# The first feed-forward block in pieces between the half images of the window attention

## What is computed

```python
h = _layernorm(x, ln1_w, ln1_b)                       # windows of 8 x 8
qkv = hw @ qkv_w + qkv_b                              # 12 heads of 8
attn = softmax(q @ k.T * scale + bias)                # per head and window
x = shortcut + (attn @ v) @ proj_w + proj_b
m = _layernorm(x, ln2_w, ln2_b)
m = gelu(m @ mlp_w1 + mlp_b1) @ mlp_w2 + mlp_b2       # 96 -> 384 -> 96
return x + m
```

## Time and profile before

| | us |
|---|---|
| median of three runs | 1312.41 |
| lowest and highest | 1305.92, 1313.32 |
| the profiled execution, its time | 1309.46 |
| its span | 1307.7 |
| window attention, from the start to 188.96 | 188.96 |
| first feed-forward program, 188.96 to 247.25 | 58.29 |
| conv mixer, 247.25 to 411.15 | 163.90 |

### The profile page before, as it was taken

How to read it: one execution, slowest core, us unless ns; L and a number is a source line. 1 busy time by engine, 2 the same in 40 slices (tenths; PEclk the granted TensorE clock), 3 DMA queues, 4 the chain that set the end, 5 groups by cost and what they waited for, 6 DMA issues and landing times. The chain is left out here.

```text
span 1307.7 us, 23695 instructions
## 1 busy us (share of the span) xinstructions
PE 1154.8 (88%) x8859; PEld 790.6 (60%) x8859; DVE 740.0 (57%) x2112; ACT 515.9 (39%) x839; POOL 387.1 (30%) x584
## 2 busy tenths in 40 slices
PE   4888879789887979999999997788888978999998
PEld 2565656566665656766666674466455544577776
DVE  3788844477772436666666666276455565333322
ACT  1555533343431333333343332345343422455543
POOL 3645445443425421010101210424100000353522
PEclk8999969899997989999999998699799999999999
DMA  4500000000000000000000000000000000000000
GB/s 88 100 11 2 2 2 0 1 1 1 2 1 1 0 1 1 1 1 1 1 1 1 1 2 1 1 1 1 1 2 1 2 2 1 2 13 7 9 11 13
DMA packets 28924, 9.39 MB, mean 7 GB/s; under 512 B 26961, under 2 KB 28816, under 8 KB 28816
## 3 DMA queue, kind: packets, MB, share of 16 engines
q1 hardware_dynamic: 25760, 7.02, 2.6%
q10 hardware_dynamic: 3056, 0.92, 0.3%
HBM read 6.36 MB, written 1.57 MB: 6 GB/s over the span
## 5 line engine op out<-in xcount | busy, mean ns | idle before, releaser
L156 POOL TENSOR_TENSOR ln_v<-MV,eps 128x2 f32<-128x2 f32 (+3 forms) x81 | 16.2, 201 | 427.2 <-PE bank L1132 247.3
L1194 ACT ACTIVATE fa_e<-bank 128x1024 f32<-128x1024 f32 x64 | 65.5, 1024 | 161.1 <-PE bank L1102 161.1
L1997 PEld LDWEIGHTS bank<-e_w,ex_G 128*128 128x128 f32 x768 | 90.6, 192 | 14.4 <-issue 14.1
L2112 DVE SCALAR_TENSOR_TENSOR X<-bank,ex_L,X 128x96 f32<-128x96 f32 x128 | 31.8, 311 | 114.0 <-PE bank L1997 108.1
L1246 DVE TENSOR_REDUCE fa_z<-bank 128x4 f32<-128x1024 f32 x64 | 78.3, 1223 | 26.3 <-PE bank L1084 24.7
L1989 PE MATMUL bank<-hT,e_w 96*128 96x512 f32 x192 | 90.6, 609 | 0.0
L1997 PE MATMUL bank<-e_w,ex_G 128*128 128x96 f32 x768 | 90.0, 274 | 0.0
L2040 ACT ACTIVATE ex_G<-bank,e_b 128x512 f32<-128x512 f32 x96 | 64.3, 686 | 61.7 <-PE bank L1989 58.9
L1844 DVE TENSOR_REDUCE ca_z<-bank 128x2 f32<-128x256 f32 x96 | 48.9, 552 | 49.3 <-PE bank L1571 49.2
L1102 PE MATMUL bank<-fa_a,fa_b 64*128 64x256 f32 x512 | 74.1, 409 | 1.1 <-DVE fa_a L1253 1.1
L1115 PE MATMUL bank<-fa_e,fa_v 128*64 128x256 f32 x512 | 72.0, 404 | 1.1 <-ACT fa_e L1194 1.1
(11 more groups left out here) (252 smaller groups left out, 2641.7 us busy)
## 6 DMA issues: line engine op xcount, KB each, us to landing
out_tokens<-X SPq DMA_DIRECT2D x8, 192.0 KB, 2.1
X<-in_x SPq DMA_DIRECT2D x56, 24.0 KB
e_w<-in_L_ffn_w SPq DMA_DIRECT2D x2, 576.0 KB
bias0r<-in_L_conv_rpb_table ACTq DMA_DIRECT2D x16, 24.0 KB
m0w<-in_L_conv_mlp_w SPq DMA_DIRECT2D x2, 144.0 KB
m1w<-in_L_conv_w SPq DMA_DIRECT2D x2, 144.0 KB
f_w<-in_L_ffn_W SPq DMA_DIRECT2D x2, 142.5 KB
mixer<-in_mixer SPq DMA_DIRECT2D x1, 256.0 KB
```

The source lines that it names most:

```text
L1194: act.activation(E[v % 2][:], k.banks[:, b:b + 2, :].rearrange("p i (c q) -> p i c q", c=2), ACT.Exp).then_inc(s["exp"], 1)
L1997: last = pe.matmul(bank[4 + e % 2][:, t * C:(t + 1) * C], G[e % 2][:, j, t * P:(t + 1) * P], k.ew2[:, e, j, :], start=(j == 0), stop=(j == ...
```

## The change

The feed-forward block's program disappears. Its work is written as four generators (`mlp_in_pieces`), whose next piece each engine's stream of the window attention calls at fixed places. From step 10 on, four steps of the attention (r = 0 to 3) hold one step m of the feed-forward block; the loop now runs to step 41. The pieces share one PSUM bank (6) and one G buffer; `probs_t` puts both of its groups into bank 2 instead. All engines wait for the late weights before step 10, GpSimd already after step 6. All statistics but those of the remaining `mlp` program are written by `bn_aggr` straight into MV, without the copy.

```diff
-def statistics(dve, k, s, n, count):
+def statistics(dve, k, s, n, count, first=0, unrolled=True):
...
+    if unrolled:
+        for t in range(count):
+            last = dve.bn_aggr(k.MV[:, n * count + t, :], k.stats[:, first + t, :])
+        last.then_inc(s["mv"], 1)
+        return
...
+def mlp_in_pieces(k, bank, ctx, prefix, w, prev):
...
+    def gpsimd(pool):
+        for i in range(IMAGES):
+            pool.wait_ge(prev["mv"], i + 1)
+            t = 4 + 2 * (i % 2)
+            normalise(pool, k, s, i, 2, k.Y[i // 2 % 2][:, t:t + 2, :], w["b2"], i // 2 - 1, 2 * i)
+            yield
...
+    def tensor(pe):
+        for m in range(steps):
+            pe.wait_ge(s["y"], 2 * m + 2)
+            after(pe, s["x"], m)
+            for t in range(4):
+                last = pe.transpose(bank[0:C, t * P:(t + 1) * P], k.Y[m % 2][:, 4 + t, :], k.ident[:])
+            last.then_inc(s["T"], 1)
+            yield
+            pe.wait_ge(s["hT"], m + 1)
+            for j in range(KH):
+                if j:
+                    pe.wait_ge(s["gelu"], KH * m + j)
+                pe.matmul(bank[:], w["w1"][:, j * P:(j + 1) * P], k.hT[m % 2][:], start=True, stop=True).then_inc(s["up"], 1)
+                yield
+            pe.wait_ge(s["gelu"], KH * (m + 1))
+            for t in range(4):
+                for j in range(KH):
+                    last = pe.matmul(bank[:, t * C:(t + 1) * C], G[:, j, t * P:(t + 1) * P], w["w2"][:, j, :], start=(j == 0), stop=(j == KH - 1))
+                if t == 1:
+                    yield
+            last.then_inc(s["down"], 1)
+            yield
+
+    def scalar(act):
+        for m in range(steps):
+            after(act, s["down"], m)
+            for j in range(KH):
+                act.wait_ge(s["up"], KH * m + j + 1)
+                act.activation(G[:, j, :], bank[:], ACT.Gelu, bias=w["b1"][:, j:j + 1]).then_inc(s["gelu"], 1)
+                yield
+
+    def vector(dve):
+        for m in range(steps):
+            dve.wait_ge(s["T"], m + 1)
+            after(dve, s["up"], KH * (m - 1))
+            dve.tensor_scalar(k.hT[m % 2][:], bank[0:C, :], w["g"][:], w["b"][:], ALU.mult, ALU.add).then_inc(s["hT"], 1)
+            yield
+            dve.wait_ge(s["down"], m + 1)
+            dve.wait_ge(s["xb"], 2 * m + 2)
+            add_new(dve, k, s, m, 4, bank[:, 0:4 * C].rearrange("p (t c) -> p t c", t=4))
+            yield
+            statistics(dve, k, s, m, 4, 2)
+            yield
...
@@ GpSimd
+                for u in range(HALVES + 6):
+                    if u < HALVES:
+                        pool.wait_ge(s["mx"], u + 1)
...
                     if u % 2 == 0 and u // 2 + 3 < IMAGES:
                         norm(u // 2 + 3)
-                pool.wait_ge(s["late"], 16 * len(k.late))
-                next_first_step(pool, k, s, IMAGES)
+                    if u == 6:
+                        pool.wait_ge(s["late"], 16 * len(k.late))
+                    if u % 2 == 1 and u >= 7:
+                        next(behind)
...
@@ TensorE, probs_t
-                    after(pe, s["pte"], 2 * u - 1 + b)
+                    after(pe, s["pte"], 2 * u + b)
...
@@ TensorE, the loop
                     if 0 <= u - 2 < HALVES:
                         probs_t(u - 2, 0)
                     if odd and 0 <= n - 2 < IMAGES:
                         outputs_t(n - 2)
+                    if r is not None:
+                        next(behind)
                     if 0 <= u - 2 < HALVES:
                         probs_t(u - 2, 1)
                     if odd and n + 2 < IMAGES:
                         queries_keys(n + 2)
+                    if r == 1:
+                        next(behind)
                     if 0 <= u - 3 < HALVES:
                         attend(u - 3)
...
+                    if r == 1:
+                        next(behind)
...
@@ ScalarE, the loop: one Gelu in r = 1 after out_t, one after pt_out(u - 2, 1), one at the end of the step
...
@@ VectorE, the loop
                     if not odd and 0 <= n - 3 < IMAGES:
                         statistics(dve, k, s, n - 3, 2)
+                    if r == 0:
+                        next(behind)
                     if 0 <= u - 3 < HALVES:
                         heads_out(u - 3)
+                    if r == 3:
+                        next(behind)
                     if odd and n + 2 < IMAGES:
                         keys_by_head(n + 2)
+                    if r == 3:
+                        next(behind)
```

More of the change, by code:

```diff
@@ L186, in statistics @@
     for t in range(count):
-        last = dve.bn_stats(k.stats[:, t, :], k.X[:, bass.ds(n * count + t, 1), :])
+        last = dve.bn_stats(k.stats[:, first + t, :], k.X[:, bass.ds(n * count + t, 1), :])
     last.then_inc(s["bn"], 1)
@@ L399, in image_stats @@
     dve.wait_ge(s[f"x{i // 4}"], 16 * 2 * WS)
+    after(dve, s["mv"], i)
     for t in range(2):
-        last = dve.bn_stats(k.stats[:, t, :], k.X[:, 2 * i + t, None, :])
+        last = dve.bn_stats(k.stats[:, 6 + t, :], k.X[:, 2 * i + t, None, :])
     last.then_inc(s["bn"], 1)
@@ L404, in image_stats @@
     for t in range(2):
[L405 to L409, removed]
+        last = dve.bn_aggr(k.MV[:, 2 * i + t, :], k.stats[:, 6 + t, :])
+    last.then_inc(s["mv"], 1)
+def mlp_in_pieces(k, bank, ctx, prefix, w, prev):
+    s = k.sems(prefix, LN_SEMS + "T hT up gelu down")
+    steps = TILES // 4
+    G = k.sb(f"{prefix}_G", [P, KH, 512], F32, ctx)
+    def gpsimd(pool):
[4 more added lines that the diff above has]
+            yield
+        count, bias = k.next_norm
+        pool.wait_ge(s["mv"], 1)
+        normalise(pool, k, s, IMAGES, count, k.Y[0][:, 0:count, :], bias, steps, 0)
+        yield
[39 more added lines that the diff above has]
+            statistics(dve, k, s, m, 4, 2)
+            yield
+    return Stage(gpsimd, tensor, scalar, vector)
@@ L421, in window_attention @@
         HALVES = 2 * IMAGES
-        FIRST, LAST = -4, HALVES + 5
+        STEPS = TILES // 4
+        FIRST, LAST = -4, HALVES + 9
+        BEHIND = 10
+        later = mlp_in_pieces(k, bank[6], ctx, "ml0", k.mlp0, s)
         bqs = sb("bqs", [C, 1])
@@ L550, in _ @@
                 pe.wait_ge(k.sem["set"]["pad"], 1)
+                behind = later.tensor(pe)
                 for u in range(FIRST, LAST + 1):
                     n, odd = u // 2, u % 2 == 1
+                    r = (u - BEHIND) % 4 if u >= BEHIND else None
+                    if u == BEHIND:
+                        pe.wait_ge(s["late"], 16 * len(k.late))
                     if 0 <= u < HALVES:
@@ L611, in _ @@
                 act.wait_ge(s["pad"], 1)
+                behind = later.scalar(act)
                 for u in range(FIRST, LAST + 1):
                     n, odd = u // 2, u % 2 == 1
+                    r = (u - BEHIND) % 4 if u >= BEHIND else None
+                    if u == BEHIND:
+                        act.wait_ge(s["late"], 16 * len(k.late))
                     if 0 <= u - 1 < HALVES:
@@ L679, in _ @@
                 next(run)
-                for u in range(FIRST, LAST + 2):
+                behind = later.vector(dve)
+                for u in range(FIRST, LAST + 1):
                     n, odd = u // 2, u % 2 == 1
+                    r = (u - BEHIND) % 4 if u >= BEHIND else None
+                    if u == BEHIND:
+                        dve.wait_ge(s["late"], 16 * len(k.late))
                     if not odd and 3 <= n + 4 < IMAGES:
@@ L751, in residual @@
                     dve.wait_ge(s["xb"], n + 1)
-                    add_and_stats(dve, k, s, n, 4, bank[7][:, 0:4 * C].rearrange("p (t c) -> p t c", t=4))
+                    add_new(dve, k, s, n, 4, bank[7][:, 0:4 * C].rearrange("p (t c) -> p t c", t=4))
+                    statistics(dve, k, s, n, 4, unrolled=False)
                 def body(n, slot, first):
@@ L2148, in build @@
         begin = setup(k, bank, a)
[L2150 removed]
+        phases = ((window_attention, (begin,), None), (conv_mixer, (), (2, k.bout)),
                   (mlp, ("ml1", k.mlp1), (4, k.mlp1["b2"])), (full_attention, (), (2, k.bp2)))
```

19 lines of the change are left out of this document (13 added, 6 removed).

## The result

The changed kernel takes 1343.94 us (median of 4 runs, 1333.04 to 1349.69), the kernel before 1309.16 (4 runs, 1300.70 to 1313.32): ratio 1.0256, 95% interval 1.0205 to 1.0308. It is slower by 34.8 us, where 13.5 were forecast.

The account below looks back on a forecast made before the run. The prediction took a TensorE-VectorE latency loop to bound the attention and TensorE the feed-forward block. 16.3 us lost up to the conv mixer less 2.8 gained behind it, 13.5, on 1309.5 gave 1323 us, range 1296 to 1346.

Parts of the forecast that it names:

- Sign and mechanism: Whole kernel slower; a merged round takes 25.35 us against 24.9 for its parts, through table loads, shared bank and VectorE's queue.
- Removed copies: Attention: VectorE's leg falls from 6.83 to about 5.6 us; conv stage: 14 images give 2.8 us; other stages: nothing.
- The start: Up to the output transposes of half step 11: they come at 91 instead of 80.93, 10 us late.
- the 10 us for the late weights: GpSimd, after half step 6, waits for weights until 74.7; half 7's subtraction, at 64.24 before, is queued behind.
- rival 4: Late weights don't hold GpSimd up, because the loads end sooner: 10 us back, 1313; chance 0.1.
- The rounds at the full clock: Four half steps with one feed-forward step take 25.35 us each; the last, lighter, 22.2.
- the clock in them: Falls to the half clock level up to the output transposes of half step 31: 3 us, giving 217.
- The tail: After half step 31, two and a half feed-forward steps: 41.5 us at full clock, 51 wholly at 1.2 GHz, 46 taken.
- The sum: Whole kernel: 16.3 us lost up to the conv mixer less 2.8 gained behind it, 13.5; 1323 us.
- Rival 2: One clock fall in each round and a tail wholly at the half level: 8 + 5 us more, 1336; chance 0.2.
- Rival 1: Engines run through each other in the merged rounds: some 21.3 us a round, 20 us back, 1303; chance 0.25.
- Rival 3: Each ScalarE table switch costs a drain as well: 16 us, 1339; chance 0.05.

Follow-up runs that it names:

- the later statistics: The changed kernel with the merged feed-forward block's statistics moved on VectorE from the end of r = 3 to r = 1 of the next round: 1326.92 us, 1.0141.
- the statistics alone: The kernel before with only bn_aggr writing straight to MV in all stages but the feed-forward programs: 1278.49 us, 0.9751.
- the one bank: The kernel before with only both groups of the probability transposes put into bank 2, bank 6 unused: 1363.47 us, 1.0402.
- the late wait in before: The kernel before with only GpSimd's wait for all late weights moved from after its last half to after half step 6: 1315.19 us, 1.0036.
- the split: The changed kernel with the six loads of the merged block's weights on their own semaphore, the rest awaited before the conv mixer: 1339.47 us, 1.0219.
- two banks: The changed kernel with the probability transposes of halves 0 to 7 in two banks as before: 1334.46 us, 1.0193.
- both together: The changed kernel with the merged block's weights on their own semaphore and two banks for halves 0 to 7: 1329.13 us, 1.0135.
- the busy tail: The changed kernel with small bf16 matmuls into idle bank 3 ahead of TensorE's waits from step 32 on: 1326.11 us, 1.0142.
- the round without table changes: The changed kernel with Identity in place of Gelu in the merged feed-forward block, so its output differs: 1315.77 us, 1.0027.
- the mended kernel: The changed kernel with own semaphore for the merged block's weights, two banks for halves 0 to 7, statistics later and small matmuls in the tail: 1310.02 us, 0.9994.

## Where the prediction held and where it failed

**Sign and mechanism: right.** The round was called no shorter than its parts, with TensorE stopped by table loads, the shared bank and VectorE's queue, and all three are there. In TensorE's idle time of after: 1.37 us at the second transposes of r = 2 (forecast 1.5), 0.80 at the second product (0.4), 1.01 at oT (2 to 2.5). Not forecast was 1.12 us at the second transposes of r = 0. The errors cancelled: 25.68 against 25.35. That VectorE's queue sets the last of them is shown by the later statistics: 1.1 us a round, and the wait gone.

**Removed copies: right in the attention and the conv mixer, missed behind them.** The leg of 8.1 us without the feed-forward pieces was measured at 8.03. The copy that ended with GpSimd's subtraction was no single case: in 13 of the 16 images of before L195 took 0.74 to 0.87 us and ended within 0.03 us of an L463, and in the last three, with no L463 beside it, 0.17. In the conv mixer the aggregates and the next product of after, which answer to the earlier trace rows, are

```profile
307.45 0.25 DVE L193 BATCH_NORM_AGGREGATE MV<-stats 128x2 f32<-128x6 f32 x2 [0.48 <-DVE stats L187]
307.62 0.45 DVE L1118 SCALAR_TENSOR_TENSOR cm_acc<-cm_g,k_conv,cm_acc 128x256 f32<-128x256 f32 x1
```

0.17 us apart instead of 0.36, and the stage is 3.0 shorter (forecast 2.8). The full attention was put at nothing, but its images start 20.65 us apart instead of 20.88, in after and with the statistics alone, at the same clock of 0.99: that is the copy's, and most of the 4.0. Its drain is another matter. The last 30.73 us of it, at a granted clock of 0.62, became 24.61 at 0.87; but the one bank and the late wait in before, which keep the copy, took 25.92 at 0.79 and 26.31 at 0.89 for the same work. So most of these 6.1 us is where the clock happened to fall in the profiled execution of before.

**The start: size nearly right, cause wrong.** oT 11 was put at 91 and came at 93.7, but the 10 us for the late weights were the wrong term. I walked the shared bank through the rounds only and left the half steps before them as they were. They have no feed-forward piece, yet they have the one bank. It alone, by its wait and by the lower clock that comes with it, delays half step 6 past the point at which the weights would stop GpSimd. The late wait in before shows that it is real (9.1 us); the split, that it is hidden in after (0.1 us); two banks, that it comes out when the bank is mended (14.8 us); and both together, that 11.2 us go only with both. Of rival 4 GpSimd's missing wait came, but not its reason, since the weights end the wait at 73.3, and not its price: nothing came back. That 93.7 lies near 91 is luck: one cost that I had left out took the place of one that I had in the sum.

**The rounds at the full clock: right; the clock in them: half.** The forecast left 3 us for falls up to oT 31; two rounds had some 3 us each. With 3 us for that, 2.7 of the start, 0.3 for each round and 1 for the last, oT 31 came at 225.2 instead of 217: 8.2 us.

**The tail: the step that failed.** "I take 46" (46.5 with the 0.5 up to the conv mixer) was between 41.5 at the full clock and "wholly at 1.2 GHz" 51, and it was 58.9: 12.4 us over. The 51 doubled only the transposes, products and w2 of two steps. The half level began at about 231, in half step 32 (229 to 233 has a granted clock of 0.64, the next 4 us 0.50), and took in the rest of the attention and part of the w2 of step 5 as well. The products L445 of the tail took up to 2.08 us, at 153.96 it had been 1.05, and the w2 of one step took 5.17 and 5.44 where the earlier trace rows has 2.91:

```profile
256.62 2.08 PE L445 MATMUL bank<-hT,m0w 96*128 96x512 f32 x2
...
259.47 5.17 PE L450 MATMUL bank<-m0w,ml_G 128*128 128x96 f32 x24 [0.78 <-ACT ml_G L461]
```

That at least 10.9 us of the 58.9 are the clock's is shown by the busy tail, 48.0 at 0.93. It also shows that the sum at the full clock was short: 48.0 against 42 (41.5 and 0.5). Of these 6 us 3.3 had come by the end of the w2 of step 5, with the half level on part of the way; the other 2.7 came behind it, at the full clock. The drain of the attention, which begins this tail, was the stretch for which the earlier trace rows had a clock of 0.58, and I took a value between the two levels when the row gave no reason to.

**The sum.** The conv mixer starts 36.6 us late where 16.3 were forecast: 8.2 + 12.4 more, less 0.3 because its first matmul in before is at 247.51 and not at 247.25. Less 0.2 in it, 4.0 in the full attention and 6.1 in its drain, that makes 23.5 in the profiled executions against 13.5. Without the luck of that drain the miss in the traces would be some 15 us and not 10. Rival 2 (the clock, 1336) is the one that came nearest: its tail for the most part at the half level, though not a fall in every round, and the tail was longer than it had priced. Rival 1 falls, since even the round without table changes and the mended kernel show no overlap that pays. Rival 3 falls as well: 0.01 us on both sides of a load. The Trainium skill ("ScalarE: Activation LUTs", What ACT_TABLE_LOAD costs) counts a drain of 1380 ns with each switch; this trace doesn't bear it out, and the kernel with both loads of a round gone is 2.5 us a round shorter, less than the two loads of 1.28 without any drain.

**What I had not asked.** What the better half would give on its own. The prediction worked out VectorE's leg without the copy and used it in the merged round only. Put into the earlier trace rows, with TensorE's 7.5 us of work, it gives images of 8.1 instead of 9.3 us: 1.2 us for each of some 14 images, 17 us. The rest of the 32 is the conv mixer and stages behind it (10.7 us in the traces, of which 5.1 lie in the drain of the full attention, at a clock of 0.89 and not 0.62) and a granted clock of 1.00 where before had 0.96.

## What to carry to other kernels

Put a work-filled loop next to its own shortened form before merging anything into it: here the stall that the merging was to fill could be removed (0.9751), and then a merged round had nothing left to fill. When a change takes a buffer away to make room for other work, walk the new wait through every step that uses the buffer, those before the merged part too, and when two new waits stand in one stretch expect to see only the longer one, and no gain from mending either alone. Where the nearest rows show the lower clock for a thinly filled tail, price all of the tail at that level.

## What the runs showed that I had not expected

- A copy of four numbers per partition on VectorE that lasts until GpSimd's subtraction ends (0.87 us in the earlier trace rows against 0.17) was worth, with the copies of its kind, 32 us of 1310.
- One shared bank made the same 1462 matmuls take 176.09 us instead of 131.47, at a granted clock of 0.66 instead of 0.93.
- Some fifty small matmuls in TensorE's waits made a tail 10.9 us shorter (58.9 to 48.0, granted clock 0.60 to 0.93) and the kernel by 1.1% (1.0142 against 1.0256; the intervals just touch). In a drain of which TensorE was not the bound they lifted the clock as well, from 0.50 to 1.00, and gave 1.3 us.
